# First edge attention of a graph network: gathers wait per half chunk, index columns copied two chunks ahead, DVE work and PE's register reads reordered

## Chip, cores, metric

One core of one Trainium2 chip runs the whole kernel. The metric is the device time of one execution in microseconds; lower is better. All times here come from runs on the chip and from one profiled execution.

## What is computed

Two layers of a graph network over 6250 nodes with 256 features and 206250 edges (src, dst), sorted by dst. The change touches only the attention over the edges in the first layer. Of the reference, this matters:

```python
q = (h @ Wq + bq).reshape(n, HD, HEADS) * scaling     # h: 6250 x 256, 8 heads of 32
k = (h @ Wk + bk).reshape(n, HD, HEADS)
v = (h @ Wv + bv).reshape(n, HD, HEADS)
s = einsum('edh,edh->eh', q[rows], k[cols])           # a score per edge and head
m = segment_max(s, rows)
e = exp(s - m[rows])
z = segment_sum(e, rows)
attn = e / z[rows]
out = segment_sum(attn[:, None, :] * v[cols], rows)   # then @ Wo + bo
```

In the attention, `rows` is dst and `cols` is src. The rest of the program (a linear attention, two mixtures of experts, a neighbour mean, a second graph attention) comes before or after it and is not touched.

## The kernel before, in words

The program is a chain of stages. `edge_attention` (line 840) is one of them; all engines join before and after it.

**Tiling.** The edges are padded into 856 steps of 256 edges, each step within one window of 128 destination nodes. A chunk is 8 steps (`CS`), that is 16 tiles of 128 edges (`CT`), and there are 107 chunks (`NCH`). The K and V rows of the 128 source nodes of a tile come by one indirect DMA (line 948) from the table `k.KV` into `kv`, which has two slots: chunk i uses slot i % 2. K takes 256 columns of a row, V takes 264 (32 and a one for each head, so that the weights are summed along with the values). The tiles of a chunk are handled in four groups g of four tiles.

**What an engine does for a chunk i.** All engines run the same loop over chunks (`chunks`, line 884: two chunks at the ends of the program unrolled, the middle a loop over pairs), and hand over by semaphores. `at(eng, sem, c, per, i)` (line 621) waits until `sem` counts c * per + i + 1: event i of chunk c, counted from 0, is done.

- *POOL* (lines 940 to 950) issues 16 gathers per chunk. Ahead of group g it waits for sum 2g+1 of chunk i-2 (`agg_ps`), which frees that part of the slot. Ahead of group 0 it also waits for `s_done`, copies the chunk's column of source indices into `idx` (two slots, line 945) and waits for that copy.
- *PE* (body at line 1084) spreads the queries of the destination nodes to the edges with one-hot matmuls (`expand`, line 1053, groups into the two halves of `psQ`); turns the scores (`turn_scores`, line 1060); sends the edge maxima of tiles across partitions (M1, line 1087; M2, line 1092); turns the exponentials (line 1099); and sums weighted values into windows (`sums`, lines 1068, 1069, 1073: three matmuls for each of the 8 steps u of a chunk, the last adding the row of `acc` that the window has so far; it raises `agg_ps`). A `sums` waits for `acc_done` of the step before, ACT's copy from PSUM to `acc` (line 988). Sums 4 to 7 of chunk i-1 stand in body i: group 2 behind M1, group 3 behind M2. Sums 0 to 3 of chunk i stand in body i, behind the turned exponentials.
- *DVE* (body at line 1197) multiplies queries by keys (`product`, line 1131) and sums over a head (`over_heads`, line 1136), giving scores S; finds the running maximum of each destination over the edges by scans (`scans`, lines 1146 to 1148), carries across tiles (`carries`, lines 1154 to 1157, after M1) and `maxima` (lines 1161 to 1171, after M2); multiplies V by the exponentials (`weigh`, line 1185); corrects the window that goes on from the chunk before (`rescale`, line 1175; `correct`, line 1192). In body i it makes products 1 to 3 of chunk i+1 last; the scores of i+1 are turned right after that.
- *ACT* makes the one-hot matrices (lines 961, 966, 977, 984), the exponentials (lines 1022, 1023), and copies sums to `acc` (line 988).
- *SP* loads the lists of relative positions, masks and flags.

Window numbers are runtime values: `windows` (line 903) reads n of them from an SBUF table into registers of an engine (line 905). PE does so five times a chunk.

The order of each engine is the order in the code; nothing plans it.

## Time and profile before

| What | Value |
|---|---|
| Median of 3 runs | 10104.04 us (10098.68 to 10116.36) |
| Profiled execution, its own time | 10101.38 us |
| Its span, first to last instruction | 10099.8 us |
| Mean granted TensorE clock | 0.799 |
| Gathers of this stage (line 948), first and last start | 896.5 and 3471.8 us |
| These 1712 gathers on POOL | 1629.4 us, 952 ns each |
| Products (line 1131), reductions (1136), weighings (1185), 428 each | 520.0, 520.0, 531.0 us of DVE |

Times in rows are microseconds from the start of the span. A timeline row gives start, duration, engine, line, operation, what is written from what, how many merged, and in brackets how long the engine was idle before it and what ended that. A matmul of float32 shows as two records.

### The profile page before, as it was taken

How to read it: one execution, taken by the hardware profiler on the slowest of the kernel's cores; microseconds unless marked ns; L12 is line 12 of the kernel's file. 1: busy time of each engine (PE TensorE's matmuls, PEld its weight loads, DVE VectorE, ACT ScalarE, POOL GpSimd, SP SyncE). 2: the span in 40 equal slices, each digit the busy share in tenths (PEclk: the TensorE clock that was granted, in tenths of full speed). 3: DMA queues.
4: the chain of work that ended last, by engine and by line, in shares of the span. 5: the costliest groups of instructions: out<-in, count | busy, mean ns of one | idle time of the engine just before them, and what ended most of it. 6: DMA issues, size and time to landing. Idle time of an engine off the chain costs nothing. (4 is left out here: it accounts for less than half of the span.)

```text
span 10099.8 us, 132193 instructions
## 1 busy us (share of the span) xinstructions
PE 6612.7 (65%) x29670; PEld 5007.3 (50%) x29671; DVE 4971.5 (49%) x10855; ACT 3047.8 (30%) x7313; POOL 6028.1 (60%) x6341
## 2 busy tenths in 40 slices
PE   4664898989889875886888555554444554555530
PEld 2333666666666664775777344443333443333320
DVE  6874777777777777665566311111111222222224
ACT  1112656666666411111222033333333211111110
POOL 1223666666666402777777377777777527777762
PEclk8777999999999997776888777777776767777765
DMA  2114766767777523222666344443333322222214
GB/s 75 50 55 156 211 206 208 209 207 209 208 209 209 168 84 99 79 79 70 179 177 176 96 120 119 119 119 101 100 101 100 87 69 44 45 44 44 44 29 159
DMA packets 657561, 1228.04 MB, mean 122 GB/s; under 512 B 165550, under 2 KB 409474, under 8 KB 657253
## 3 DMA queue, kind: packets, MB, share of 16 engines
q0 software_dynamic: 301872, 718.92, 25.9%
q1 hardware_dynamic: 327959, 467.65, 14.9%
q10 hardware_dynamic: 27580, 39.79, 1.1%
q8 instruction: 55, 0.90, 0.0%
q14 instruction: 95, 0.78, 0.0%
HBM read 1088.88 MB, written 145.05 MB: 122 GB/s over the span
## 5 line engine op out<-in xcount | busy, mean ns | idle before, releaser
L948 POOL DMA_INDIRECT e_kv<-KV,e_idx x1712 | 1629.4, 952 | 760.7 <-issue 483.4
L2469 POOL DMA_INDIRECT s_x<-XN,s_idx x1712 | 1621.3, 947 | 589.7 <-issue 500.8
L2526 PE MATMUL s_psA<-s_x,s_oh 128*128 128x256 f32 x1712 | 664.4, 477 | 1112.7 <-DMA s_x<-XN,s_idx 1022.1
L1593 POOL DMA_INDIRECT SD<-o_pay,o_pos x1024 | 1077.9, 1053 | 360.3 <-issue 314.6
L2884 POOL DMA_INDIRECT t_g<-G,t_idx x1088 | 1076.1, 989 | 329.6 <-issue 329.6
L2562 DVE TENSOR_TENSOR NS<-s_psA,NS 128x256 f32 x856 | 363.7, 425 | 1743.3 <-PE s_psA L2527 1742.9
L1053 PE MATMUL e_psQ<-QA,e_oht 128*128 x3424 | 893.7, 407 | 200.7 <-issue 115.8
L2526 PEld LDWEIGHTS s_psA<-s_x,s_oh 128*128 128x128 f32 x1712 | 405.9, 245 | 1222.7 <-issue 1152.5
L1053 PEld LDWEIGHTS e_psQ<-QA,e_oht 128*128 128x128 f32 x3424 | 646.7, 199 | 367.8 <-issue 281.4
L3052 PE MATMUL t_psH<-t_xT,t_w 128*128 128x384 f32 (+1 forms) x1088 | 425.4, 558 | 378.8 <-ACT t_H L3029 358.2
L988 ACT ACTIVATE QA<-e_psA 128x264 f32 x856 | 332.0, 388 | 996.1 <-PE e_psA L1073 986.2
L2527 PE MATMUL s_psA<-s_x,s_oh 128*128 128x256 f32 x1712 | 625.5, 453 | 0.0
L1131 DVE TENSOR_TENSOR e_kv<-e_psQ,e_kv 128x1024 f32<-128x1024 f32 x428 | 520.0, 1215 | 102.1 <-PE e_psQ L1053 48.0
L1073 PE MATMUL e_psA<-QA,ident 128*128 x1712 | 564.0, 411 | 0.0
L1068 PE MATMUL e_psA<-e_kv,hold 128*128 128x264 f32 x1712 | 544.4, 400 | 11.9 <-issue 7.2
L977 ACT ACTIVATE hold<-iota,e_relt 128x128 f32<-128x128 f32 x1712 | 542.1, 388 | 18.4 <-ACT e_relt L971 10.7
L1136 DVE TENSOR_REDUCE e_S<-e_kv 128x32 f32<-128x1024 f32 x428 | 520.0, 1215 | 32.0
L1185 DVE TENSOR_TENSOR e_kv<-e_psP,e_kv 128x1056 f32<-128x1056 f32 x428 | 531.0, 1241 | 0.2 <-PE e_psP L1099 0.2
L2488 ACT ACTIVATE s_oh<-iota,s_relt 128x128 f32<-128x128 f32 x1712 | 517.4, 387 | 39.0 <-PE s_psA L2527 29.7
L1069 PE MATMUL e_psA<-e_kv,hold 128*128 128x264 f32 x1712 | 522.8, 387 | 0.0
L3052 PEld LDWEIGHTS t_psH<-t_xT,t_w 128*128 128x128 f32 x1088 | 239.0, 224 | 561.7 <-issue 360.9
L2527 PEld LDWEIGHTS s_psA<-s_x,s_oh 128*128 128x128 f32 x1712 | 407.8, 238 | 82.4
(580 smaller groups left out, 12424.9 us busy)
## 6 DMA issues: line engine op xcount, KB each, us to landing
o_dbf<-DBF SPq DMA_DIRECT2D x128, 512.0 KB
f_w<-in_L_ffn_Wd_dram SPq DMA_DIRECT2D x57, 1024.0 KB
e_relb<-REL SPq DMA_DIRECT2D x107, 512.0 KB, 5.9
o_dlo<-DLO SPq DMA_DIRECT2D x128, 256.0 KB
e_kv<-KV,e_idx POOLq DMA_INDIRECT x1712, 3.8
s_x<-XN,s_idx POOLq DMA_INDIRECT x1712, 2.8
YD<-t_y ACTq DMA_DIRECT2D x50, 512.0 KB, 2.7
mx_y<-YD SPq DMA_DIRECT2D x10, 2560.0 KB, 12.4
```

The costliest lines, as they stand in the source:

```text
L948: pool.indirect_dma_start(kv[:, s, t, :], None, k.KV, bass.IndirectOffsetOnAxis(ap=idx[:, s, t:t + 1], axis=0)).then_inc(kv_in[s][g], 16)
L977: last = act.activation(oh[:, s, t, :], k.iota[:], ACT.Abs, bias=relt[:, s, t:t + 1])
L1053: last = pe.matmul(psQ[:, g % 2, t % 4, :], oht[:, s, t * P:(t + 1) * P], acc[:, bass.ds(b[t // 2 % 4] + 1, 1), 0:C].rearrange("p a n -> p ...
L1068: pe.matmul(psA[:, u % 2, 0:VW], oh[:, s, 2 * u, :], kv[:, s, 2 * u, C:KW], start=True, stop=False)
L1073: pe.matmul(psA[:, u % 2, 0:VW], k.ident[:], acc[:, bass.ds(r[u % 4], 1), :].rearrange("p a n -> p (a n)"), start=False, stop=True).then_i ...
L1185: dve.tensor_tensor(v, p, v, ALU.mult).then_inc(pv_done, 1)
L1593: pool.indirect_dma_start(self.k.SD, bass.IndirectOffsetOnAxis(ap=self.pos[:, s, j:j + 1], axis=0), self.pay[:, s, j, :], None).then_inc(s ...
L2469: pool.indirect_dma_start(x[:, s, t, :], None, k.XN2, bass.IndirectOffsetOnAxis(ap=idx[:, s, t:t + 1], axis=0)).then_inc(x_in[s], 16)
L2526: pe.matmul(psA[:, u % 4, 0:C], oh[:, o, 2 * u, :], x[:, s, 2 * u, :], start=True, stop=False)
L2527: pe.matmul(psA[:, u % 4, 0:C], oh[:, o, 2 * u + 1, :], x[:, s, 2 * u + 1, :], start=False, stop=True)\
L2884: pool.indirect_dma_start(g[:, s, j, :], None, k.G, bass.IndirectOffsetOnAxis(ap=idx[:, s, j:j + 1], axis=0)).then_inc(g_in[s], 16)
L3052: last = pe.matmul(psH[:, m % 2, 0:n * P], w1[:, a, m * P:(m + 1) * P], xT[:, a, 0:n * P], start=(a == 0), stop=(a == KC - 1))
```

## The change

- `gather` waits twice per chunk instead of four times: ahead of tiles 0 to 7 for sum 3 of chunk i-2 (counted from 0, so the fourth), ahead of tiles 8 to 15 for sum 7 (the eighth). The wait for `s_done` goes.
- `idx` has four slots. The columns of chunk i+2 are copied within chunk i, between the second wait and gather 8. The POOL loop now runs over four chunks.
- PE's register reads are moved: each stands between the two steps of a `sums` (or ahead of the wait for `x1_done`), one use ahead.
- DVE does `weigh(i-1, 3)` ahead of `carries`, `product(i+1, 0)` ahead of `maxima`, and `over_heads(i+1, 0)` ahead of `rescale`.

```diff
--- before.py
+++ after.py
@@ -843,6 +843,7 @@
 
     scale = float(DK) ** -0.5
     LINKS = 10
+    IS = 4
     with ExitStack() as c:
         sb = lambda name, shape, dt=F32: c.enter_context(nc.sbuf_tensor("e_" + name, shape, dt))
         sem = semaphores(nc, c, before="e_")
@@ -852,7 +853,7 @@
         oh = k.hold[:, 0:2 * CT * P].rearrange("p (s t n) -> p s t n", s=2, t=CT)
         t3 = k.hold[:, 2 * CT * P:2 * CT * P + 2 * TW].rearrange("p (s f) -> p s f", s=2)
         flg = sb("flg", [HEADS, 2, CT + 1, 4])
-        idx = sb("idx", [P, 2, CT], I32)
+        idx = sb("idx", [P, IS, CT], I32)
         relt = sb("relt", [P, 2, CT])
         S = sb("S", [P, CT, HEADS])
         FL = sb("FL", [P, 2 * P])
@@ -937,17 +938,28 @@
             pool.memset(acc[:, 0, :], 0.0).then_inc(zeroed, 1)
             pool.memset(acc[:, 1:NT + 1, C:VW], 0.0).then_inc(zeroed, 1)
 
-            def gather(i, s):
-                for g in range(4):
-                    at(pool, agg_ps, i - 2, CS, 2 * g + 1)
-                    if g == 0:
-                        at(pool, s_done, i - 2, 4, 3)
-                        pool.tensor_copy(idx[:, s, :], k.src_i[:, bass.ds(i * CT, CT)]).then_inc(idx_done, 1)
-                        at(pool, idx_done, i, 1, 0)
-                    for t in range(4 * g, 4 * g + 4):
-                        pool.indirect_dma_start(kv[:, s, t, :], None, k.KV,
-                                                bass.IndirectOffsetOnAxis(ap=idx[:, s, t:t + 1], axis=0)).then_inc(kv_in[s][g], 16)
-            chunks(pool, gather)
+            def columns(i, n):
+                pool.tensor_copy(idx[:, n, :], k.src_i[:, bass.ds(i * CT, CT)]).then_inc(idx_done, 1)
+
+            def gather(i, n):
+                s = n % 2
+                at(pool, idx_done, i, 1, 0)
+                for h in range(2):
+                    at(pool, agg_ps, i - 2, CS, CS // 2 * h + CS // 2 - 1)
+                    if h == 1 and inside(i + 2):
+                        columns(i + 2, (n + 2) % IS)
+                    for t in range(8 * h, 8 * h + 8):
+                        pool.indirect_dma_start(kv[:, s, t, :], None, k.KV, bass.IndirectOffsetOnAxis(ap=idx[:, n, t:t + 1], axis=0))\
+                            .then_inc(kv_in[s][t // 4], 16)
+            columns(0, 0)
+            columns(1, 1)
+            for i in range(IS):
+                gather(i, i)
+            with pool.Fori(1, NCH // IS - 1) as j:
+                for n in range(IS):
+                    gather(IS * j + n, n)
+            for i in range((NCH // IS - 1) * IS, NCH):
+                gather(i, i % IS)
 
         @block.scalar
         def _(act):
@@ -1059,11 +1071,18 @@
                 at(pe, x3_done, i - 1, 1, 0)
                 pe.transpose(ST, S[:].rearrange("p t h -> p (t h)"), k.ident[:]).then_inc(st_ps, 1)
 
-            def sums(i, s, g, r):
-                at(pe, pv_done, i, 4, g)
-                if g % 2 == 0:
-                    at(pe, oh_done, i, 2, g // 2)
-                for u in (2 * g, 2 * g + 1):
+            def spread_windows(i, half):
+                return windows(mybir.EngineType.PE, i * CS + 4 * half, 4)
+
+            def sum_rows(i, half):
+                return windows(mybir.EngineType.PE, i * CS + 4 * half, 4, k.step_r)
+
+            def sums(i, s, g, r, us=(0, 1)):
+                if 0 in us:
+                    at(pe, pv_done, i, 4, g)
+                    if g % 2 == 0:
+                        at(pe, oh_done, i, 2, g // 2)
+                for u in (2 * g + v for v in us):
                     at(pe, acc_done, i, CS, u - 2)
                     pe.matmul(psA[:, u % 2, 0:VW], oh[:, s, 2 * u, :], kv[:, s, 2 * u, C:KW], start=True, stop=False)
                     pe.matmul(psA[:, u % 2, 0:VW], oh[:, s, 2 * u + 1, :], kv[:, s, 2 * u + 1, C:KW], start=False, stop=False)
@@ -1082,18 +1101,28 @@
             expand(1, 1, 0, windows(mybir.EngineType.PE, CS, 4))
 
             def body(i, s):
-                more = inside(i + 1)
+                more, old = inside(i + 1), not first_of(i)
+                if old:
+                    r = sum_rows(i - 1, 1)
                 at(pe, x1_done, i, 1, 0)
                 pe.matmul(M1, k.selh[:], rhs1[:].rearrange("p a t -> p (a t)"), start=True, stop=True).then_inc(m1_ps, 1)
-                if not first_of(i):
-                    r = windows(mybir.EngineType.PE, i * CS - 4, 4, k.step_r)
-                    sums(i - 1, 1 - s, 2, r)
+                if old:
+                    sums(i - 1, 1 - s, 2, r, (0,))
+                if more:
+                    b = spread_windows(i + 1, 0)
+                if old:
+                    sums(i - 1, 1 - s, 2, r, (1,))
                 at(pe, x2_done, i, 1, 0)
                 pe.matmul(M2, k.selT[:], rhs2[:].rearrange("p a t -> p (a t)"), start=True, stop=True).then_inc(m2_ps, 1)
-                if not first_of(i):
-                    sums(i - 1, 1 - s, 3, r)
+                if old:
+                    sums(i - 1, 1 - s, 3, r, (0,))
+                now = sum_rows(i, 0)
+                if old:
+                    sums(i - 1, 1 - s, 3, r, (1,))
+                r = now
                 if more:
-                    expand(i + 1, 1 - s, 1, windows(mybir.EngineType.PE, i * CS + CS, 4))
+                    expand(i + 1, 1 - s, 1, b)
+                    b = spread_windows(i + 1, 1)
                 at(pe, exp_done, i, 1, 0)
                 at(pe, pv_done, i - 1, 4, 3)
                 pe.transpose(psP[:, 0:P], E[:], k.ident[:]).then_inc(p_ps, 1)
@@ -1101,20 +1130,22 @@
                 pe.matmul(FAC, k.ones[0:1, :], k.ones[0:1, 0:HEADS], start=True, stop=False)
                 pe.matmul(FAC, ohrow[:], gm[:], start=False, stop=True).then_inc(fac_ps, 1)
                 if more:
-                    b = windows(mybir.EngineType.PE, i * CS + CS + 4, 4)
                     expand(i + 1, 1 - s, 2, b)
-                r = windows(mybir.EngineType.PE, i * CS, 4, k.step_r)
                 sums(i, s, 0, r)
                 if more:
                     expand(i + 1, 1 - s, 3, b)
-                sums(i, s, 1, r)
+                sums(i, s, 1, r, (0,))
+                if inside(i + 2):
+                    b = spread_windows(i + 2, 0)
+                sums(i, s, 1, r, (1,))
                 if more:
                     turn_scores(i + 1)
                 if inside(i + 2):
-                    expand(i + 2, s, 0, windows(mybir.EngineType.PE, i * CS + 2 * CS, 4))
+                    expand(i + 2, s, 0, b)
                 if last_of(i):
+                    r = sum_rows(i, 1)
                     for g in range(2, 4):
-                        sums(i, s, g, windows(mybir.EngineType.PE, i * CS + g // 2 * 4, 4, k.step_r))
+                        sums(i, s, g, r)
             chunks(pe, body)
 
         @block.vector
@@ -1201,15 +1232,14 @@
                 scans(i, s)
                 if old:
                     weigh(i - 1, 1 - s, 2)
+                    weigh(i - 1, 1 - s, 3)
                 carries(i, s)
-                if old:
-                    weigh(i - 1, 1 - s, 3)
+                if more:
+                    product(i + 1, 1 - s, 0)
                 maxima(i, s)
                 if more:
-                    product(i + 1, 1 - s, 0)
+                    over_heads(i + 1, 1 - s, 0)
                 rescale(i)
-                if more:
-                    over_heads(i + 1, 1 - s, 0)
                 weigh(i, s, 0)
                 correct(i, b)
                 weigh(i, s, 1)
```

## Rows read from the trace of the kernel before

**Rows 1.** Windows, first 1000 us of the stage (stretch, busy us and instructions by engine):

```profile
core 0: us, PE busy (x) PEld busy (x) DVE busy (x) ACT busy (x) POOL busy (x), PEclk, DMA share, GB/s
1000.00:2000.00 1000.00, 902.50 (x3766) 663.95 (x3765) 761.21 (x1210) 603.52 (x1383) 644.15 (x710) 0.98 0.70 208
```

**Rows 2.** Line 1060, from 1000 to 3400 us:

```profile
L1060 PEld LDWEIGHTS e_psX<-ident,e_S x100: 137/138/142, 1019.1 to 3386.4; 128*128 128x128 f32 x100
```

**Rows 3.** Timeline of PE, one chunk:

```profile
2049.22 0.30 PE L1060 MATMUL e_psX<-ident,e_S 128*128 128x128 f32 x1 [0.80 <-DVE e_S L1136]
2050.27 1.99 PE L1053 MATMUL e_psQ<-QA,e_oht 128*128 x8 [0.75 <-issue]
...
2052.66 0.68 PE L1068 MATMUL e_psA<-e_kv,hold 128*128 128x264 f32 x2 [0.25 <-issue]
...
2055.05 0.71 PE L1073 MATMUL e_psA<-QA,ident 128*128 x2
...
2058.43 0.71 PE L1073 MATMUL e_psA<-QA,ident 128*128 x2
...
2066.63 0.71 PE L1073 MATMUL e_psA<-QA,ident 128*128 x2
...
2071.21 0.71 PE L1073 MATMUL e_psA<-QA,ident 128*128 x2
2072.72 0.30 PE L1060 MATMUL e_psX<-ident,e_S 128*128 128x128 f32 x1 [0.81 <-DVE e_S L1136]
```

**Rows 4.** Timeline of DVE, the same chunk:

```profile
2047.75 1.22 DVE L1136 TENSOR_REDUCE e_S<-e_kv 128x32 f32<-128x1024 f32 x1
...
2050.85 1.25 DVE L1185 TENSOR_TENSOR e_kv<-e_psP,e_kv 128x1056 f32<-128x1056 f32 x1
2052.52 0.24 DVE L1154 TENSOR_TENSOR_SCAN e_xs<-e_flg,e_xs,e_psX 8x16 f32<-8x16 f32 x1 [0.42 <-PE e_psX L1087]
...
2056.20 0.19 DVE L1161 TENSOR_TENSOR e_junk<-e_psX,maskj 128x32 f32<-128x32 f32 x1 [1.62 <-PE e_psX L1092]
...
2061.10 0.21 DVE L1175 SCALAR_TENSOR_TENSOR e_gm<-ident,e_fx 8x8 f32<-8x8 f32 x1 [0.69 <-ACT e_fx L1023]
...
2062.37 1.24 DVE L1185 TENSOR_TENSOR e_kv<-e_psP,e_kv 128x1056 f32<-128x1056 f32 x1
...
2069.94 1.22 DVE L1131 TENSOR_TENSOR e_kv<-e_psQ,e_kv 128x1024 f32<-128x1024 f32 x1
```

**Rows 5.** Timeline of POOL, the same chunk:

```profile
2056.53 0.94 POOL L948 DMA_INDIRECT e_kv<-KV,e_idx  x1 [1.66 <-PE e_psA L1073]
...
2065.29 0.95 POOL L948 DMA_INDIRECT e_kv<-KV,e_idx  x1 [0.30 <-issue]
2067.69 0.19 POOL L945 COPY e_idx<-src_i 128x16 int32 x1 [1.46 <-DVE e_S L1136]
2068.67 0.98 POOL L948 DMA_INDIRECT e_kv<-KV,e_idx  x1 [0.78 <-POOL e_idx L945]
```

**Rows 6.** The gathers, line 948, from 1000 to 3400 us: who waited, and landing:

```profile
  DVE e_kv L1131: 5.5, 11
...
DMA to landing us min/median/max: 3.3/3.8/5.6
```

**Rows 7.** Register reads of PE, line 905:

```profile
L905 PEldq TENSOR_LOAD <-step_i x320: 327/332/517, 933.1 to 3467.9; - x160
```

**Rows 8.** Waits from 1000 to 3400 us (who waited for whom: us, times, longest):

```profile
PEld e_psA L1073 <- issue: 133.6, 402, 0.4
...
DVE e_xs L1154 <- PE e_psX L1087: 95.0, 100, 2.3
```

**Rows 9.** Windows, the 3.4 us behind the transposition at 2024.49 (columns of rows 1):

```profile
2025.30:2028.70 3.40, 3.12 (x7) 2.52 (x8) 1.80 (x4) 1.71 (x2) 2.49 (x4) 0.50 0.75 217
```

**Rows 10.** Timeline of PE, the chunk before that of rows 3:

```profile
2024.49 0.30 PE L1060 MATMUL e_psX<-ident,e_S 128*128 128x128 f32 x1 [1.36 <-DVE e_S L1136]
2025.58 3.53 PE L1053 MATMUL e_psQ<-QA,e_oht 128*128 x8 [0.79 <-issue]
...
2034.99 0.71 PE L1073 MATMUL e_psA<-QA,ident 128*128 x2
```

## What the change should do to the time

> **What bounds the kernel now.** The change lies in one function, so I first asked the two windows what that stage does: no engine is full. In 1000 us of it PE is busy 902.50, DVE 761.21, POOL 644.15 us, and the DMA engines 0.70 of the time [rows 1]. So the order of waits sets the pace. The period comes from the score transposition (line 1060), once per chunk: its 100 starts run from 1019.1 to 3386.4, (3386.4 - 1019.1) / 99 = 23.91 us a chunk [rows 2]. Then the timeline of one undisturbed chunk. I count t from the transposition at 2049.22; the next is at 2072.72, a period of 23.50 [rows 3]. DVE is dense from its first weighing (t+13.15) to its last reduction; before that it waits three times for PE: 0.42 for M1, 1.62 for M2, 0.69 for the exponential [rows 4]. DVE and PE together set the period, by passing scans, carries, maxima and exponential to and fro.
>
> POOL is close behind. Its gathers stand 1.25 us apart, eight of them from the first start to the last 8.76 (2056.53 to 2065.29), and it waits twice: 1.66 us before gather 8, 1.46 before the index copy [rows 5]. The first of these waits is for the sixth sum of the chunk two back (line 1073): that ends at 2055.05 + 0.71 = 2055.76, t+6.54 [rows 3], and gather 8 starts 0.77 later. The eighth sum ends at 2058.43 + 0.71 = 2059.14, t+9.92, 3.38 later; today the gathers that need it come long after. The last product of the chunk starts at 2069.94, 4.65 after the last gather [rows 4, 5]. A gather lands 3.8 us after its issue (median) [rows 6]. So the gathers have only 4.65 - 3.8 = 0.85 us to spare, and DVE waits for them 11 times, 5.5 us in all [rows 6].
>
> **Part 1, waits per half chunk.** The second half of the gathers of a chunk now waits for sum 8 instead of sum 6 of the chunk two back; that is 3.38 us later against 0.85 us of slack. What is queued behind the wait on POOL: the index copy, the eight gathers, and the next chunk's first half. Who waits: DVE's products 2 and 3, through them the transposition, PE, and so sum 8 of the next chunk. This closes a loop inside one period. Today's terms, as a check: 6.54 (to sum 6) + 0.77 + 8.76 + 4.65 + 2.78 (last product to next transposition, 2069.94 to 2072.72) = 23.50, the measured period.
>
> The first half waits for sum 4 instead of sum 2: 2071.92 instead of 2067.34 [rows 3], 4.58 us later. Its own loop is worked out under the rivals; it comes out shorter.
>
> **Part 2, index columns.** Removed from the front of a chunk: the copy (0.19) and the wait for its semaphore (0.78), and the redundant wait on s_done [rows 5]. They are hidden: POOL has to wait for its sum there anyway. Added ahead of the second half: a copy between the wait and gather 8. A copy starts 0.35 us after the sum it waited for (2067.34 to 2067.69), lasts 0.19, and the usual gap to a gather is 0.30: 0.84, with one register operation 0.9, instead of 0.77 [rows 3, 5]. Bounds: 0.77 (copy hidden) and 0.35 + 0.19 + 0.78 = 1.32 (as today's copy and gather). I take 0.9, since the following gather waits for no semaphore of this copy.
>
> **Part 3, register reads on PE.** After the transposition PE sat 0.75 us before expanding [rows 3], and a read takes 0.33 [rows 7]; with its setup I take 0.5 off (bounds 0.33 and 0.75). The expansion and M1 come 0.5 earlier. The sums behind M1 cannot: they need the weighing that ends at 2050.85 + 1.25 = 2052.10 [rows 4], plus 0.25 for the hand-over (2048.97, the end of the reduction, to 2049.22 in [rows 3, 4]), 2052.35 instead of 2052.66. So sum 8 gains 0.3 and ends at t+9.6. The reads that moved between two sums lie beside the matmuls of the first, and beside the wait that each second sum has for ACT's copy of the one before: line 1073 stood idle 402 times for that, 133.6 us, 0.33 each, four times a chunk [rows 8]. They cost nothing; if that cover were gone, some 0.33 for each of the reads [rows 7].
>
> **Part 4, DVE's order.** Weighing 3 moves ahead of the carries and product 0 ahead of the maxima. DVE's wait for M1 (0.42) and most of that for M2 (1.62) fill up: weighing 3 ends at t+4.1, carries at t+5.05, product 0 at t+6.3, M2's result is there at t+6.7 instead of t+6.98. Behind the maxima a product of 1.2 us is gone, but the exponential is late next (ready t+11.6), so the first weighing comes at t+12.1 instead of t+13.15 [rows 4]. By itself this saves 1.05 us a chunk. On the path to sum 8 it saves nothing: that path is transposition, expansion, M1, sums, M2, sums, all PE.
>
> **The sum.** New period: 9.6 (to sum 8) + 0.9 + 8.76 + 3.8 + 2.78 = 25.84 us in an undisturbed chunk. Part 4's gain goes into DVE's wait before products 2 and 3: product 3 can start at t+23.06, and DVE would have come to it at about t+19.67 (20.72 today, less 1.05).
>
> **The clock** comes on top. The granted clock has a mean of 0.98 [rows 1]; but in the chunk before the one read above, 3.4 us behind the transposition ran at 0.50, 1.2 GHz instead of 2.4 [rows 9], and the eight expansion records took 3.53 instead of 1.99 us [rows 3, 10]. It fell after PE's longest pause, 1.36 us before the transposition at 2024.49; with 0.80 and 0.81 us it did not [rows 3, 10]. DVE's wait for M1 has a mean of 95.0 / 100 = 0.95 [rows 8], 0.53 over the 0.42 of this chunk [rows 4]; at 3.53 - 1.99 = 1.54 for a slow one that makes a third of the chunks. In a slow chunk sum 8 ended at 2034.99 + 0.71 = 2035.70, t+11.21 [rows 10]; with 0.5 off for the read (the weighing no longer holds it) t+10.7, a period of 10.7 + 16.25 = 26.95. Now PE's pause before each transposition grows to about 25.84 - 22.1 = 3.7 us (sum 4 ends today at t+22.70, and 0.6 sooner by parts 3 and 4), nearly three times the one that brought the drop. I expect a drop in every chunk, now and then partly within the pause, and take 26.8.
>
> The Trainium skill bears on that: TensorE: Matmul & The Clock Gate, section "HAM oscillation — how this bites in real kernels", says in my words that a loop whose matmuls wait for a transfer each time starts each burst at the low clock. The trace so far shows it for one chunk in three only. By that rule every chunk would pay in full, 26.95 us and 104 x 3.04 = +316 us, which I count to the forecast, at its slow side; by the share that the trace has now the mean would be 25.84 + 1.1 / 3 = 26.2.
>
> The first two chunks wait for no sums, which leaves 104 periods or so: 104 x (26.8 - 23.91) = +300 us. The profiled execution took 10101.4; it becomes 10402. The median of the runs is 2.7 us above it: 10404, said as **10400 us**. Nothing outside the stage changes.
>
> **Rivals.**
> - *Clock as now* (same loop, drops in a third of the chunks or fewer): 26.2, or 25.84 with none. 104 x 2.3 = +239 and +202: 10340 and 10306. For it: two pauses of three bring no drop today. Against it: those are pauses of 0.8 us, not 3.7. Chance 0.2.
> - *Both bounds high*: the copy costs 1.32 and the drop in full, 27.4 us: +360, 10465. Chance 0.07.
> - *The first half decides, the second is hidden.* Sum 4 to the product 0 that needs gathers 0 to 3: 0.77 + 3.75 + 3.8 = 8.32; product 1.2; from the maxima to sum 4 today 2071.92 - 2056.20 = 15.72, less 1.05: together 24.2, +0.3 us a chunk, 10135. Against it: 24.2 is less than 25.84, and the longer loop wins. Chance 0.03.
> - *Faster: DVE and PE set the period and the gathers stay hidden.* Place: product 3. Then part 4 is worth 1.05 us a chunk: 104 x 1.05 = -109, 9995. It decides only if the last gather lands before t+19.6, so if sum 8 came by t+6.1; it comes at t+9.6. A shorter landing helps little: the minimum is 3.3 instead of 3.8 [rows 6]. Chance 0.05. This is also where it ends if the half-chunk wait did not hold back gather 8 as its count says.
>
> The forecast has 0.65. Within it, the bounds of copy (0.13 less, 0.4 more), read and drop move the period by -0.6 to +0.5 us, 10340 to 10455. The range for 8 in 10 takes in most of the clock rival: **10300 to 10450**. A difference of 0.2% (20 us) is about what a measurement of this kernel can tell from none. Faster 0.05, within 0.2% 0.02, slower 0.93.
>
> **What would show it.** Right: period of line 1060 near 26.8; product 3 (line 1131) waits for the DMA of e_kv in nearly every chunk, with product 2 some 2 to 3.5 us; gather 8 starts 0.8 to 1.3 after sum 8, and the last gather to product 3 is 3.8; DVE's waits for M1 and M2 nearly gone; the granted clock of the stage near 0.94 instead of 0.98. Wrong: product 3 without a wait for DMA; a gather 8 that starts before sum 8; a period below 24; a product 0 that waits for DMA longer than product 3 (then the first half decides).

## The result, and the profile after

Before took 10104.35 us (median of 4 runs, 10098.68 to 10116.36), the changed kernel 10479.24 us (4 runs, 10468.68 to 10488.23): a ratio of 1.0369, with an interval of 1.0351 to 1.0387. The change costs 375 us. The forecast was 10400 with a range of 10300 to 10450: the direction and the mechanism came out, the time lies 29 us above the range. The profiled execution took 10481.98 us, its span is 10480.4.

First the page: busy time by engine, and the costliest group of instructions:

```profile
PE 6745.8 (64%) x29670; PEld 5111.1 (49%) x29671; DVE 5001.6 (48%) x10855; ACT 3049.8 (29%) x7313; POOL 6025.7 (57%) x6341
...
L952 POOL DMA_INDIRECT e_kv<-KV,e_idx x1712 | 1621.9, 947 | 832.3 <-issue 529.5
```

The work itself is unchanged: as many gathers as before. What changed is when they start. The transposition's line, now 1072, from 1000 to 3400 us:

```profile
L1072 PEld LDWEIGHTS e_psX<-ident,e_S x88: 137/139/184, 1001.2 to 3387.9; 128*128 128x128 f32 x88
```

(3387.9 - 1001.2) / 87 = 27.43 us a chunk, where [rows 2] gave 23.91. The expectation was 26.8. 104 periods of 3.52 us more are 366 us, nearly the whole loss; the stage is longer by 372 us of the 381 by which the spans differ.

The waits of all engines over the same stretch (who waited for whom: us, times, longest):

```profile
POOL e_idx L942 <- PE e_psA L1092: 401.4, 85, 7.3
...
PE e_psX L1072 <- DVE e_S L1167: 365.7, 86, 5.6
DVE e_kv L1162 <- DMA e_kv<-KV,e_idx: 316.3, 181, 3.8
POOL e_kv L952 <- PE e_psA L1092: 216.3, 88, 7.4
...
DVE e_junk L1192 <- PE e_psX L1116: 105.8, 85, 2.1
...
DVE e_xs L1185 <- PE e_psX L1108: 33.5, 77, 0.5
```

Read this list as a circle. POOL waits for PE's sums (lines 942 and 952, 401.4 and 216.3 us). DVE waits for what POOL fetched: 316.3 us in 181 waits, where [rows 6] had 5.5 us in 11. PE waits for DVE's last reduction ahead of each transposition, 4.25 us on average. Each engine waits for the next one in the ring, and none is full.

One chunk shows the ring at work. The timeline of PE (start, duration, engine and line, and in brackets the idle time before it and who ended it):

```profile
2069.12 0.30 PE L1072 MATMUL e_psX<-ident,e_S 128*128 128x128 f32 x1 [4.13 <-DVE e_S L1167]
2069.66 3.59 PE L1065 MATMUL e_psQ<-QA,e_oht 128*128 x8 [0.25 <-issue]
...
2079.16 0.71 PE L1092 MATMUL e_psA<-QA,ident 128*128 x2
...
2091.41 0.71 PE L1092 MATMUL e_psA<-QA,ident 128*128 x2
2096.39 0.30 PE L1072 MATMUL e_psX<-ident,e_S 128*128 128x128 f32 x1 [4.27 <-DVE e_S L1167]
```

POOL in the same chunk:

```profile
2080.10 0.19 POOL L942 COPY e_idx<-src_i 128x16 int32 x1 [4.64 <-PE e_psA L1092]
2080.79 0.98 POOL L952 DMA_INDIRECT e_kv<-KV,e_idx  x1 [0.49 <-issue]
...
2089.57 0.95 POOL L952 DMA_INDIRECT e_kv<-KV,e_idx  x1 [0.30 <-issue]
2092.90 0.94 POOL L952 DMA_INDIRECT e_kv<-KV,e_idx  x1 [2.38 <-PE e_psA L1092]
```

And DVE, its four products (line 1162) and the first use of M2 (line 1192):

```profile
2074.55 1.22 DVE L1162 TENSOR_TENSOR e_kv<-e_psQ,e_kv 128x1024 f32<-128x1024 f32 x1
2076.93 0.19 DVE L1192 TENSOR_TENSOR e_junk<-e_psX,maskj 128x32 f32<-128x32 f32 x1 [1.16 <-PE e_psX L1116]
...
2089.03 1.23 DVE L1162 TENSOR_TENSOR e_kv<-e_psQ,e_kv 128x1024 f32<-128x1024 f32 x1 [1.48 <-DMA e_kv<-KV,e_idx]
...
2093.59 1.22 DVE L1162 TENSOR_TENSOR e_kv<-e_psQ,e_kv 128x1024 f32<-128x1024 f32 x1 [2.02 <-DMA e_kv<-KV,e_idx]
```

From transposition to transposition: sum 8 ends at 2079.16 + 0.71 = 2079.87 (t+10.75), gather 8 starts 0.92 later, the last gather 8.78 after it (2089.57), product 3 after 4.02 (2093.59), and the next transposition after 2.80 (2096.39). The sum is 27.27, this chunk's period exactly. Product 0, at 2074.55, waits for no transfer: the first half of the gathers is early enough.

The clock, by windows (us, then busy time of PE, PEld, DVE, ACT and POOL with their instructions, the clock, the DMA share and GB/s): the 1000 us of [rows 1], then this chunk's first 3.4 us and its remainder:

```profile
1000.00:2000.00 1000.00, 830.56 (x3291) 610.88 (x3289) 675.98 (x1064) 529.65 (x1209) 561.42 (x622) 0.91 0.62 182
2069.90:2073.30 3.40, 3.40 (x10) 2.21 (x9) 2.99 (x5) 0.00 (x0) 2.49 (x4) 0.50 0.76 202
2073.30:2097.20 23.90, 19.06 (x83) 14.37 (x82) 15.55 (x25) 14.51 (x33) 13.04 (x15) 1.00 0.61 181
```

After PE's pause of 4.13 us the clock stands at 0.50 (1.2 GHz) for 3.4 us, and the eight expansion records take 3.59 us instead of 1.99 [rows 3]. This now happens in every chunk, where before it was one in three (30 of chunks 5 to 100); the mean over these 1000 us fell from 0.98 to 0.91. The eight records took 3.19 to 3.78 us in each of chunks 5 to 100. By the Trainium skill, TensorE: Matmul & The Clock Gate, section "HAM oscillation — how this bites in real kernels", a loop whose matmuls wait for a transfer in every pass starts each burst at the low clock. The trace of the changed kernel agrees, in 96 chunks of 96.

Means of the terms over chunks 5 to 100, each beside the forecast's:

| term, us | forecast | measured |
|---|---|---|
| transposition to end of sum 8 | 9.6, or 10.7 with the drop | 10.88 |
| sum 8 to gather 8 | 0.9 | 0.90 |
| gather 8 to the last gather | 8.76 | 8.90 |
| last gather to product 3 | 3.8 | 3.96 |
| product 3 to the next transposition | 2.78 | 2.80 |
| period | 26.8 | 27.45 |

### The profile page after: what moved, and what is told of

Same layout as the page of the kernel before. It is cut to its first block and busy times, and to the rows that moved or that the text cites. A ratio compares the mean times of both kernels' runs of the same rounds, so it can differ in the third digit from the quotient of the medians.

```text
span 10480.4 us, 131316 instructions
## 1 busy us (share of the span) xinstructions
PE 6745.8 (64%) x29670; PEld 5111.1 (49%) x29671; DVE 5001.6 (48%) x10855; ACT 3049.8 (29%) x7313; POOL 6025.7 (57%) x6341
## 5 line engine op out<-in xcount | busy, mean ns | idle before, releaser
L1065 PE MATMUL e_psQ<-QA,e_oht 128*128 x3424 | 1013.1, 448 | 76.2 <-ACT e_oht L978 56.9
L1065 PEld LDWEIGHTS e_psQ<-QA,e_oht 128*128 128x128 f32 x3424 | 726.7, 221 | 242.5 <-issue 122.1
L989 ACT ACTIVATE hold<-iota,e_relt 128x128 f32<-128x128 f32 x1712 | 542.0, 388 | 18.4 <-ACT e_relt L983 10.7
```

Source lines behind the costliest of these rows:

```text
L989: last = act.activation(oh[:, s, t, :], k.iota[:], ACT.Abs, bias=relt[:, s, t:t + 1])
L1065: last = pe.matmul(psQ[:, g % 2, t % 4, :], oht[:, s, t * P:(t + 1) * P], acc[:, bass.ds(b[t // 2 % 4] + 1, 1), 0:C].rearrange("p a n -> p ...
```

## The experiments

Theory: the second half's wait for sum 8 closes the loop above; of the rest of the change little can be seen because of it. Rivals: the first half's wait for sum 4 carries the loss; or a part other than the waits does (the clock by itself, the moved reads, DVE's order).

Nearly every run has to be read with one reservation. The chips were met in two conditions: in one the kernel before took 10104 to 10121 us, as in the result, in the other 12070 to 12255 us. Below they are called the 10.1 ms and the 12.1 ms condition. Each ratio is against the kernel before on the same chip in the same condition, but the theory's sizes were worked out for the 10.1 ms condition, and the last part of this document shows how different the other one is. The table has all runs, the five of the 10.1 ms condition first:

| run | before, us | run, us | ratio, interval |
|---|---|---|---|
| control_before | 10109.26 | 10104.86 | one execution |
| control_after | 10109.26 | 10478.12 | 1.0364, 1.0347 to 1.0382 |
| half_waits_alone_2 | 10108.09 | 10528.58 | 1.0409, 1.0389 to 1.0430 |
| both_split_4 | 10120.67 | 10039.75 | 0.9921, 0.9905 to 0.9938 |
| pair_waits_2 | 10116.46 | 9979.98 | 0.9870, 0.9854 to 0.9886 |
| second_half_split | 12225.60 | 12547.48 | 1.0267, 1.0238 to 1.0296 |
| first_half_split | 12225.60 | 12172.89 | 0.9958, 0.9937 to 0.9978 |
| both_split | 12225.60 | 12210.55 | 0.9984, 0.9969 to 0.9999 |
| warm_pause | 12225.60 | 12694.44 | 1.0388, 1.0364 to 1.0413 |
| second_half_split_2 | 12227.13 | 12551.11 | 1.0258, 1.0239 to 1.0276 |
| both_split_2 | 12227.13 | 12224.12 | 0.9995, 0.9983 to 1.0007 |
| second_half_split_3 | 12069.61 | 12469.01 | 1.0332, 1.0315 to 1.0350 |
| both_split_3 | 12069.61 | 12070.18 | 1.0000, 0.9987 to 1.0013 |
| half_waits_alone | 12069.61 | 12354.68 | 1.0241, 1.0204 to 1.0277 |
| second_half_split_4 | 12070.79 | 12457.03 | 1.0317, 1.0300 to 1.0334 |
| warm_pause_2 | 12229.61 | 12728.68 | 1.0412, 1.0392 to 1.0431 |
| pair_waits | 12074.56 | 11969.00 | 0.9921, 0.9894 to 0.9949 |
| second_half_split_5 | 12255.29 | 12560.90 | 1.0250, 1.0225 to 1.0275 |

**The two kernels again.** In the first runs before took 12226 and 12227 us, so both kernels were run unchanged once more.

> The kernel before, unedited, for its profile on such a chip (12227 us instead of 10104). If the chip is slower everywhere alike, every duration in the stage is some 20% longer. If single pauses make it, the durations are those of the trace of before, and the period of line 1060 in this stage is above 23.91 us by pauses of several us that no wait for another engine's work explains, as in second_half_split. The loop of the second half (sum 6 to gather 8 in 0.77 us, 1.25 us a gather, 3.8 us to land) keeps its terms.

> The changed kernel, unedited, beside the kernel before on such a chip. Theory (the second half's wait closes a loop of 27.4 us): where the period is already longer than 27.4 us for another reason, the loop costs less or nothing, so the ratio is below the 1.037 of the prediction's chip, near 1.00 to 1.02. If the change itself does more work or the other parts cost time, the ratio stays near 1.037.

Before took 10104.86 us, after 10478.12, a ratio of 1.0364. The ring has the same terms: sum 8 at t+10.92, then 0.90, product 3 3.95 behind the last gather, 2.80, a period of 27.48. The result repeats to 0.05%. Both expectations were written for the 12.1 ms condition; it wasn't there, so their ratio of 1.00 to 1.02 is not tested by this.

**All four waits back, the rest of the change kept.** The changed kernel, but POOL waits ahead of tiles 0, 4, 8 and 12 for sums 2, 4, 6 and 8, as before; the columns are copied ahead of tile 12:

```diff
-                for h in range(2):
-                    at(pool, agg_ps, i - 2, CS, CS // 2 * h + CS // 2 - 1)
-                    if h == 1 and inside(i + 2):
+                for first, end, u in [(0, 4, 1), (4, 8, 3), (8, 12, 5), (12, 16, 7)]:
+                    at(pool, agg_ps, i - 2, CS, u)
+                    if u == CS - 1 and inside(i + 2):
                         columns(i + 2, (n + 2) % IS)
-                    for t in range(8 * h, 8 * h + 8):
+                    for t in range(first, end):
```

> The same kernel as both_split, alone on its chip beside the kernel before. Only if the kernel before takes about 10105 us here does it test the theory: 22.8 to 23.5 us a chunk, 9985 to 10060. Rival 2 (order on DVE and reads cost time): 25 us a chunk or more, 10200 or more. If the gathers still bind a little: 23.5 to 23.9, 10060 to 10105. If the kernel before takes some 12100 us, both again within 0.3% of each other.

10039.75 us, a ratio of 0.9921, within the theory's 9985 to 10060: parts 2 to 4 by themselves gain 81 us. The transposition's line, the waits of the products for the gathers (us, times), both from 1000 to 3300 us, and the window:

```profile
L1072 PEld LDWEIGHTS e_psX<-ident,e_S x99: 137/138/142, 1020.3 to 3295.4; 128*128 128x128 f32 x99
```

```profile
  DMA e_kv<-KV,e_idx: 28.2, 58
```

```profile
1000.00:2000.00 1000.00, 906.66 (x3866) 675.34 (x3867) 791.25 (x1248) 621.97 (x1420) 663.39 (x732) 0.99 0.73 215
```

The period is (3295.4 - 1020.3) / 98 = 23.22 us and the clock 0.99: the drop is left in 9 of chunks 5 to 100, where before had 30. In the chunks without it sum 8 ends at t+9.79 on average, and at t+9.81 in those of before: part 3 is worth nothing there. The first weighing starts at t+12.28 in these chunks, at t+13.02 in those of before: part 4 is worth some 0.7 at that place. Little of that reaches the period of such a chunk, 23.15 against 23.46 us; the rest of the gain is that dropped chunks are fewer and shorter, 23.90 against 24.96 us. Three earlier runs of the same kernel, in the 12.1 ms condition, showed no difference of a size to speak of:

> The changed kernel with all four waits as before (sums 2, 4, 6, 8 ahead of each four tiles), the index columns still copied two chunks ahead, and the rest of the change kept. Theory: both gather loops are out of the way, DVE and PE set the period, and what parts 3 and 4 save shows: 22.8 to 23.5 us a chunk, 9985 to 10060, faster than the kernel before. Rival 1: the same. Rival 2 (order on DVE and reads cost time): 25 us a chunk or more, 10200 or more. If the gathers still bind a little, between 23.5 and 23.9, and 10060 to 10105.

> The same kernel as both_split, again, for the same reason. Theory: 22.8 to 23.5 us a chunk, 9985 to 10060, faster than before. Rival 2 (order on DVE and reads cost time): 25 us a chunk or more, 10200 or more. If the gathers still bind a little: 23.5 to 23.9, 10060 to 10105.

> The same kernel as both_split, for such a chip. Theory: 22.8 to 23.5 us a chunk, 9985 to 10060, faster than before. Rival 2: 25 us a chunk or more, 10200 or more. If the gathers still bind a little: 23.5 to 23.9, 10060 to 10105.

0.9984, 0.9995 and 1.0000. In that condition the gain of 81 us isn't to be had, but the main statement stands: without the half-chunk waits the loss is gone.

**The half-chunk waits alone.** The kernel before with part 1 only:

```diff
-                    at(pool, agg_ps, i - 2, CS, 2 * g + 1)
+                    if g % 2 == 0:
+                        at(pool, agg_ps, i - 2, CS, 2 * g + 3)
```

> The same kernel as half_waits_alone (part 1 alone on the kernel before), alone on its chip, for a chip where the kernel before takes about 10110 us. Theory: sum 8 ends at t+9.92, or 11.3 with the drop of the clock in every chunk, then 0.77 + 8.9 + 3.95 + 2.8: 26.3 to 27.7 us a chunk, 10350 to 10500; part 1 alone carries the whole loss. Rival (the loss comes from the other parts, or only from all together): within 50 us of 10110.

10528.58 us, a ratio of 1.0409. The same three views, line 1061 being its transposition and 1132 its product:

```profile
L1061 PEld LDWEIGHTS e_psX<-ident,e_S x83: 137/138/183, 1000.2 to 3294.1; 128*128 128x128 f32 x83
```

```profile
  DMA e_kv<-KV,e_idx: 218.4, 155
```

```profile
1000.00:2000.00 1000.00, 820.60 (x3218) 600.75 (x3218) 655.54 (x1041) 512.93 (x1175) 548.27 (x607) 0.91 0.61 178
```

So part 1 by itself carries the whole loss, and 420 us of it, 45 more than the full change. The period is (3294.1 - 1000.2) / 82 = 27.97, the clock 0.91 as in the changed kernel. Both lie a little above the expectation (27.7 us, 10500). The ring has one longer and one shorter term: sum 8 ends at t+11.52 instead of 10.88, and gather 8 follows after 0.83 instead of 0.90. The difference of some 0.55 us a chunk is what parts 2 to 4 still give inside the ring: 0.64 less 0.07 for the copy and 0.02 in the gathers. Of the 0.64, 0.51 is the read that no longer stands ahead of an expansion at half clock: that starts at t+0.55 instead of t+1.06. DVE's shorter order gives nothing there; it only lengthens DVE's wait for the gathers.

This trace also tells the two halves apart. Gather 8 starts 0.78 to 0.89 us after sum 8 in each of chunks 5 to 100, so nothing but sum 8 holds it. Product 0 starts 9.98 us behind gather 3 on average and never less than 8.07, product 1 10.86 behind gather 7 and never less than 8.98, where 3.96 is all that a product needs behind its last gather. So the first half, though it too waits for a whole half, lies off the path in every chunk, and the loss here is the second half's.

An earlier run of this kernel was in the 12.1 ms condition:

> The kernel before with part 1 alone: it waits ahead of gather 0 for sum 4 and ahead of gather 8 for sum 8 (the index copy, DVE's order and the register reads as before). Theory: sum 8 ends at t+9.92, or 11.3 with the drop of the clock that the longer pause brings, then 0.77 + 8.9 + 3.95 + 2.8: 26.3 to 27.7 us a chunk, 10350 to 10500; it carries the whole loss and more. Rival (the loss comes from the other parts, or only from all together): within 50 us of 10105.

1.0241, 285 us of loss. The direction agrees.

**One half at a time.** `second_half_split` gives the second half its two waits back and keeps the first half's single one, `first_half_split` the other way about; the edit is the one above, with these lists:

```diff
+                for first, end, u in [(0, 8, 3), (8, 12, 5), (12, 16, 7)]:   # second_half_split
+                for first, end, u in [(0, 4, 1), (4, 8, 3), (8, 16, 7)]:     # first_half_split
```

> The changed kernel, but the second half of the gathers waits twice again: tiles 8 to 11 for sum 6, tiles 12 to 15 for sum 8 (the index copy moves ahead of tile 12). The first half still waits once, for sum 4. Theory (the loop sum 8, gathers 8 to 15, product 3 sets the changed kernel's 27.44 us a chunk): that loop loses 3.38 us and ends below the next one, so the period falls to the loop of the first half, 24.2 to 25.0 us; time 10100 to 10225. Rival 1 (the first half's wait decides): 27.4 us, 10480 as the changed kernel. Rival 2 (the order on DVE and the moved register reads cost the time): 27 us or more, 10440 or more.

> The changed kernel, but the first half of the gathers waits twice again: tiles 0 to 3 for sum 2, tiles 4 to 7 for sum 4; the second half waits once, for sum 8. Theory (second half decides): nothing changes, 27.4 us a chunk and 10480, within 20 us. Rival 1 (first half decides): 25 us or less, below 10230. Rival 2 (order on DVE and reads): 10480 too, so this run does not tell it from the theory.

> The same kernel as second_half_split, again, since the kernel before took 12226 us on the chip of that run, 2100 us more than on the chip of the prediction, with pauses of up to 8 us in which no engine's wait was for work of another. On a chip where the kernel before takes about 10104 us. Theory (second half's wait decides the changed kernel): 24.2 to 25.0 us a chunk, 10100 to 10225. Rival 1 (first half decides): 27.4 us a chunk, 10480. Rival 2 (order on DVE and reads): 27 us or more, 10440 or more.

> The same kernel as second_half_split, for a chip on which the kernel before takes about 10105 us. Theory (second half's wait decides the changed kernel): its loop loses 3.38 us, the first half's loop is next; from the changed kernel's trace, sum 4 to gather 0 0.78, three gathers 3.75, landing 3.9, product 1.3, maxima to sum 4 15.2 or less: at most 24.9 us a chunk, at least 23.5; 10060 to 10215. Rival 1 (first half decides): 27.4 us, 10480. Rival 2 (order on DVE and reads cost time): 27 us or more, 10440 or more.

> The same kernel as second_half_split, alone on its chip, for a chip where the kernel before takes about 10110 us. Theory (second half's wait decides the changed kernel): its loop loses 3.4 us and the first half's loop is next: sum 4 to gather 0 0.78, three gathers 3.75, landing 3.9, product 1.3, maxima to sum 4 14.5 to 15.2, in all 24.3 to 25.0 us a chunk, 10130 to 10215. Rival 1 (the first half's wait decides the changed kernel): 27.4 us, 10480.

> The same kernel as second_half_split, once more for a chip on which the kernel before takes about 10110 us. Theory (second half's wait decides the changed kernel, the first half's loop is next): 24.3 to 25.0 us a chunk, 10130 to 10215. Rival 1 (the first half decides): 27.4 us, 10480.

This went against the theory: 1.0267, 1.0258, 1.0332, 1.0317 and 1.0250 with the second half split, 0.9958 with the first half split. In these runs it is the first half's wait that costs. But all six were in the 12.1 ms condition, and their ring is another one: in the last of them sum 4 ends at t+33.8 of a 34.1 us chunk and gather 0 follows 0.78 later; product 0 starts 3.97 behind gather 3, no more than product 3 has in the closed ring above, so it is product 0 that is late; product 3 has 6.98, three more than it needs. In the changed kernel in the 10.1 ms condition it is the reverse: product 3 at 3.96, product 0 at 5.07. No run with one half split was made in that condition, so how much each of the two waits carries in the changed kernel is not shown by an experiment. What puts it on the second there are two traces, that of the changed kernel and, more plainly, that of half_waits_alone_2 above.

**The clock.** The changed kernel with 13 matmuls that nobody reads, in PE's pause ahead of the transposition, to keep the clock up:

```diff
+                    for _ in range(13):
+                        pe.matmul(psP[:, P:2 * P], k.ident[:], k.ident[:], start=True, stop=True)
```

> The changed kernel with 13 matmuls of 128 columns whose result nobody reads (identity times identity, into unused columns of psP) ahead of each transposition of the scores, some 2.8 us of work in PE's pause; the output stays the reference's. If the clock's drop after the pause is part of the changed kernel's period, as the sum has it (sum 8 at t+10.88 instead of t+9.6), the drop goes and the period falls by 1.3 us to 26.1: 10340. If the price of the drop is hidden, the time stays at 10480. The granted clock of the stage, 0.91 in the changed kernel, rises towards 1.00 in both cases.

> The same kernel as warm_pause (the changed kernel with 13 matmuls in PE's pause), alone on its chip, for a chip where the kernel before takes about 10110 us. If the drop of the clock is part of the changed kernel's period: sum 8 ends at t+9.8 (both_split_4 has it there without drops) instead of t+10.88, the period falls by 1.1 us to 26.4, the time by 110 us to 10370. If its price is hidden: 10480. The stage's granted clock rises from 0.91 to near 1.00 in both cases.

1.0388 and 1.0412, neither near the expectation, again with before at 12226 and 12230 us, and without a run of the changed kernel in that condition to set beside them. The trace of warm_pause shows why the run is no use: PE is busy with the 13 matmuls until the transposition in every chunk, and this comes 5.14 us behind product 3 instead of 2.80. So they lengthen the path. The expansion behind it ran at the full clock in all chunks (1.89 to 1.99 us), yet the clock over 1000 to 2000 us was 0.89: it falls elsewhere. This says nothing of the drop's price. The price can be read otherwise, from two traces with the same instructions on PE: sum 8 ends at t+10.88 in the changed kernel and at t+9.79 in the chunks of both_split_4 without a drop, so a drop costs 1.1 us. Over all chunks of both_split_4 the mean is t+9.88; the 1.0 us a chunk between the two kernels is 104 us of the 440 by which they differ, and the rest is the wait itself. This is a reading, not an experiment.

**Finer waits than before.** If the wait for a whole half is what hurts, a wait for each pair of tiles should help. Eight waits a chunk, each for the one sum that frees the next two tiles, the copy ahead of tile 14:

```diff
+                for u in range(CS):
+                    at(pool, agg_ps, i - 2, CS, u)
+                    if u == CS - 1 and inside(i + 2):
+                        columns(i + 2, (n + 2) % IS)
+                    for t in range(2 * u, 2 * u + 2):
```

> The other way round: as both_split, but POOL waits ahead of each two tiles for the one sum that frees them (eight waits a chunk; the index copy ahead of tile 14). In both_split_4 the last gather to product 3 is 4.16 us in the mean and 3.83 at least, so the gathers still bind in part of the chunks. With these waits gather 8 starts after sum 5 instead of sum 6, 1.5 us sooner. Theory: the gathers are out of the way, DVE alone is left, at both_split_4's fastest chunks, 22.57 to 22.8 us a chunk instead of 23.22; 104 x 0.5 = 50 us less, 9970 to 10005. Rival (the four more waits cost POOL what they gain, or DVE and PE bind): 10035 to 10045 as both_split_4.

> The same kernel as pair_waits, for a chip on which the kernel before takes about 10110 us (it took 12075 in pair_waits, with a ratio of 0.992). Theory: gathers out of the way, 22.57 to 22.8 us a chunk instead of both_split_4's 23.22, 9970 to 10005, ratio 0.986 to 0.990. Rival (the four more waits cost what they gain, or DVE and PE bind at 23.2): 10035 to 10050, ratio 0.992 to 0.994.

0.9921 in the 12.1 ms condition, and 9979.98 us, 0.9870, in the 10.1 ms condition: within the theory's 9970 to 10005, faster than both kernels, 136 us below before.

```profile
L1072 PEld LDWEIGHTS e_psX<-ident,e_S x101: 137/139/142, 1019.8 to 3286.9; 128*128 128x128 f32 x101
```

```profile
  DMA e_kv<-KV,e_idx: 0.7, 2
```

```profile
1000.00:2000.00 1000.00, 922.24 (x3970) 687.99 (x3970) 805.71 (x1282) 636.80 (x1454) 677.80 (x749) 1.00 0.74 220
```

The period is (3286.9 - 1019.8) / 100 = 22.67 us, the last gather now lies 5.24 us ahead of product 3, where [rows 4, 5] had 4.65, DVE waits for gathers twice in all, and the clock is 1.00. This is the rival "DVE and PE set the period and the gathers stay hidden": 23.91 - 22.67 = 1.24 us a chunk, against the 1.05 that it was given. The two are not quite the same thing: without a drop a chunk of before takes 23.46 us, so 0.79 is the shorter order, and 0.45 the drop that no chunk has any more. Six us of waits in 2400 [rows 6] had seemed to leave finer waits nothing to win, but with both_split_4 DVE waited 28.2 us in 58 waits: once parts 3 and 4 shorten the rest, before's own grain is the next limit, and 0.55 us a chunk (23.22 - 22.67) comes from going below it, 0.07 of that because the last dropped chunks go.

## Why the prediction missed its range

- **Part 1, the loop: right.** Gather 8 waits for sum 8, product 3 waits for the last gather in every chunk, and the four other terms of the ring are where they were put. Part 1 alone brings the loss, taking it back removes it. DVE's waits for the gathers came to 316.3 / 88 = 3.6 us a chunk, a little over the "some 2 to 3.5". The first half was rightly told to be the shorter loop: product 0 has 5.07 us behind gather 3 and needs about 3.9; this is read from traces, as said above.
- **Part 2, the copy: right.** 0.90 us from sum 8 to gather 8, forecast 0.9 between bounds of 0.77 and 1.32. The rival "both bounds high" (10465) is the nearest in time, but for another reason: its copy wasn't the dear one.
- **Part 3, the reads: half right, and here the sum failed first.** "So sum 8 gains 0.3 and ends at t+9.6" did not come: with the clock up it ends at t+9.79 (both_split_4), against 9.81 in such chunks of before. The step took the weighing's end plus 0.25 for the hand-over, a figure from a reduction to a transposition; from the weighing's end to the sums it is 0.50 in both kernels. With the drop the read does gain: 10.88 on average (10.75 in the chunk shown) instead of 11.30 in the dropped chunks of before, or 11.52 in half_waits_alone_2; forecast 10.7. Short by 0.19 in the clean ring and by 0.18 in the dropped one.
- **Part 4, DVE's order: right in kind, too large.** 0.7 us instead of 1.05, and M2 is still waited for: 105.8 us in 85 waits, 1.24 each, where "nearly gone" was written. M1's wait did go (33.5 us, of 95.0 in [rows 8]). As forecast, none of it reaches the period while the ring is closed.
- **The transfer: short by 0.16.** 3.8 is the median from issue to landing. The ring has 3.96 from the start of the last gather to the product that waits for it.
- **The gathers: short by 0.14.** 8.76 was one undisturbed chunk. The mean in the kernel before was 8.88 already, since now and then one gather comes late by 1.4 us; in a closed ring those chunks count in full.
- **The clock: right in result and price, a little low in share, and partly by luck.** Each chunk drops in full, not "now and then partly within the pause". That choice was 26.8 instead of 26.95. A drop costs 1.1 us, as it was put; the clock over 1000 us is 0.91, not the 0.94 forecast. But the rows that the step leaned on, a drop behind a pause of 1.36 us and none behind 0.80 and 0.81, were three chunks that happened to lie so. Of the 30 chunks with a drop among chunks 5 to 100 of before, 25 follow a pause of at most 0.84 us, and 7 pauses of over 1.2 us have none behind them.

With the drop in full the steps as written gave 26.95, measured are 27.45. The 0.50 between them are 0.18 + 0.00 + 0.14 + 0.16 + 0.02 over the five terms: sum 8, copy, gathers, landing, last stretch. 104 x 0.65 = 68 us, from 26.8 on; 8 us more lie outside the stage. The traces of the 10.1 ms condition have 7488 to 7500 us there with the same code, so these 8 need no cause in the change. 10402 + 68 + 8 = 10478, for a profiled execution of 10482.

So the mechanism, its place and its sign were right, and the step that failed is the sum's sizes: sum 8 with the drop (10.88 for 10.7), the gathers (8.90 for 8.76), the landing (3.96 for 3.8), and the 0.15 taken off for partial drops. The first three were taken from one chunk or from a median, and each came out above it. In a ring of five terms such errors don't cancel. The upper end of the range, 10450, came from adding single bounds to a centre that was itself a best case.

## What to carry to other kernels

Before a release wait is made coarser, lay the time by which it comes later beside the slack of the last transfer that hangs on it (here 3.38 us against 0.85): whatever exceeds the slack is paid in every iteration, because the late consumer delays the next release. The other direction is worth trying even when the waits look small: eight waits a chunk instead of four gained 1.3% together with the other edits, 0.55 us a chunk of it by the waits; on POOL, which waits anyway, the four more waits cost nothing that shows. To price a closed ring, take means over all iterations, not a clean one, and add the lower clock where PE's new pause brings one.

## What the runs showed beyond the forecast

- **The same kernel in two conditions of a chip.** Before took 10104 to 10121 us in one and 12070 to 12255 in the other. Chip 10 showed both: 10109 with the controls, 12075 with pair_waits. It isn't of this stage alone: the rest of the program takes 7488 to 7500 us in the traces of the one and 8872 us in second_half_split_5. SyncE's own small instructions are the plainest sign. The per-chunk load of `e_flg`, in control_before (min/median/max ns):

```profile
L921 SPq FUSED_REGOPS  x102: 37/40/47, 987.6 to 3404.9; - x102
L921 SPq MOVE e_flg<-FLG x102: 29/29/29, 987.7 to 3405.0; - x102
```

and in second_half_split_5, with the longest of its waits from 1000 to 3400 us:

```profile
L922 SPq FUSED_REGOPS  x102: 5/699/910, 990.0 to 4441.2; - x102
L922 SPq MOVE e_flg<-FLG x102: 5/691/728, 990.7 to 4441.9; - x102
```

```profile
PEld e_psA L1092 <- issue: 699.1, 336, 10.0
ACT QA L1000 <- remote: 662.4, 92, 10.1
```

A register move takes 691 ns instead of 29, and ACT stands still for up to 10 us with nothing in the trace that it waited for. The chunk becomes 31 to 35 us long, and which wait ends last changes with it. What brings this about is open. It puts the ratios of that condition out of use for a theory of sizes, and there the wait of the other half is the one that costs (second_half_split).

- **The clock and PE's pause.** The pause of some 4.2 us ahead of the transposition was followed by a clock of 0.50 in each chunk, for 3.4 us in the one shown. A closed ring thus pays twice: for the transfer, and 1.1 us more for PE's slow start behind it. Yet the length of that pause alone doesn't decide. In the kernel before it was 85.0 us in 96 waits (0.89 each, up to 1.7), with a drop in one chunk of three; in both_split_4 it is longer and there is hardly a drop:

```profile
PE e_psX L1072 <- DVE e_S L1167: 102.8, 99, 2.4
```

1.04 us each, up to 2.4, at a clock of 0.99 (from 1000 to 3300 us, as for the kernel before). PE's pauses elsewhere in the chunk differ too, by parts 3 and 4; which of them spare the drop wasn't tried.
